# The front of the first feed-forward in smaller pieces, with its third batch mixed in the attention's tail

## What is computed

```python
x = x + _L0_attn_ref(_layernorm(x, axis=-1), ...)   # 16 heads of 8, rotary, masked by pages of 32 tokens, then @ wo
x = x + _L0_ffn_ref(_layernorm(x, axis=-1), ...)

def _L0_ffn_ref(x, gate_w, w1, b1, w2, b2, w3, b3, sw1, sw2, sw3):
    logits = xt @ gate_w.T
    scores = jax.nn.softmax(logits.astype(jnp.float32), axis=-1)
    top_vals, idx = jax.lax.top_k(scores, K)                  # K = 2 of E = 8 experts
    xs = xt[:, None, :] * weights[:, :, None]
    for e in range(E):
        mask = (idx == e).astype(x.dtype)
        h = jax.nn.silu(jnp.einsum('tkd,hd->tkh', xs, w1[e]) + b1[e])
        x2 = jnp.einsum('tkh,dh->tkd', h, w2[e]) + b2[e]
        x3 = jnp.einsum('tkd,hd->tkh', xs, w3[e]) + b3[e]
        y = y + jnp.sum(x2 * x3 * mask[:, :, None], axis=1)
    z = jax.nn.silu(xt @ sw1.T) * (xt @ sw2.T) @ sw3.T
    return (y + z).reshape(B, S, D)
```

## Time and profile before

| | |
|---|---|
| median of 3 runs | 1481.11 us (1480.87 to 1486.27) |
| the profiled execution | 1482.99 us, of which the span 1481.1 us |
| TensorE busy | 1214.6 us, 82% of the span |
| VectorE busy | 1153.7 us, 78% |
| ScalarE busy | 672.6 us, 45% |
| POOL busy | 653.5 us, 44% |
| mean granted TensorE clock | 0.907 of full speed |
| DMA | 120.37 MB, mean 81 GB/s |

### The profile page before, as it was taken

How to read it: one execution, slowest core, us unless ns; L and a number is a source line. 1 busy time by engine, 2 the same in 40 slices (tenths; PEclk the granted TensorE clock), 3 DMA queues, 4 the chain that set the end, 5 groups by cost and what they waited for, 6 DMA issues and landing times. The chain is left out here.

```text
span 1481.1 us, 21354 instructions
## 1 busy us (share of the span) xinstructions
PE 1214.6 (82%) x7478; PEld 548.8 (37%) x7478; DVE 1153.7 (78%) x1366; ACT 672.6 (45%) x1057; POOL 653.5 (44%) x468
## 2 busy tenths in 40 slices
PE   4937999998999789879978767877877867766998
PEld 2412334333344344444444212322322322355565
DVE  5868999998996256747556889999999999964554
ACT  2515999997897413212215783333333323302221
POOL 2320000101002166636743068989989989921000
PEclk9956999999999889989997868999999999995999
DMA  4321111312101443313520013343333333400331
GB/s 105 121 94 44 57 50 51 115 48 77 50 25 46 103 112 112 110 57 105 120 50 18 6 51 128 128 128 104 117 119 128 128 100 115 126 9 24 68 57 43
DMA packets 75346, 120.37 MB, mean 81 GB/s; under 512 B 13246, under 2 KB 42758, under 8 KB 75254
## 3 DMA queue, kind: packets, MB, share of 16 engines
q1 hardware_dynamic: 75254, 119.16, 27.2%
HBM read 105.09 MB, written 13.63 MB: 80 GB/s over the span
## 5 line engine op out<-in xcount | busy, mean ns | idle before, releaser
L635 DVE TENSOR_REDUCE att_found<-PS 128x2 f32<-128x1024 f32 (+2 forms) x288 | 333.2, 1219 | 17.9 <-PE PS L738 16.1
L705 ACT ACTIVATE att_prob<-PS 128x512 f32<-128x512 f32 x576 | 313.6, 596 | 42.5 <-PE PS L760 30.5
L1694 PE MATMUL PS<-ms_ch,ident_sb 128*128 128x512 f32 x512 | 269.0, 651 | 72.6 <-POOL ms_ch L1801 72.6
L1801 POOL TENSOR_TENSOR ms_ch<-xnT,ms_c_rows 128x1024 f32<-128x1024 f32 x128 | 304.8, 2392 | 41.3 <-DVE xnT L1759 21.3
L1759 DVE TENSOR_TENSOR_SCAN xnT<-ms_decay,PS 128x1024 f32<-128x1024 f32 x96 | 216.1, 2276 | 4.2
L779 PE MATMUL PS<-att_prob,att_v 128*32 128x256 f32 (+1 forms) x2560 | 183.9, 374 | 2.8 <-ACT att_out L694 2.6
L1694 PEld LDWEIGHTS PS<-ms_ch,ident_sb 128*128 128x128 f32 x512 | 98.6, 204 | 194.8 <-POOL ms_ch L1801 107.5
L1732 ACT ACTIVATE PS<-m_dt,m_a 128x1024 f32<-128x1024 f32 x32 | 35.8, 1118 | 260.5 <-DVE xnT L1759 260.5
L738 PE MATMUL PS<-kr,qr 55*128 55x128 bf16 (+4 forms) x1152 | 121.4, 292 | 30.8 <-PEq L260 15.6
L760 PE MATMUL PS<-qr,kr 55*128 55x128 bf16 (+4 forms) x1152 | 115.3, 278 | 15.5 <-ACT att_prob L705 9.1
L1746 DVE TENSOR_TENSOR PS<-ms_dtu,PS 128x1024 f32<-128x1024 f32 x96 | 114.7, 1213 | 6.8 <-PE PS L1685 6.7
(11 more groups left out here) (222 smaller groups left out, 1632.5 us busy)
## 6 DMA issues: line engine op xcount, KB each, us to landing
ms_c_rows<-bc_rows_dram SPq DMA_DIRECT2D x64, 512.0 KB, 5.9
f_gate_row<-gate_rows_dram SPq DMA_DIRECT2D x64, 256.0 KB, 3.4
ms_b_row<-bc_rows_dram SPq DMA_DIRECT2D x32, 512.0 KB, 3.6
f_mask_row<-mask_rows_dram SPq DMA_DIRECT2D x64, 128.0 KB, 3.0
qk_parts_dram<-qkv_parts SPq DMA_DIRECT2D x48, 128.0 KB, 1.9
heads_dram<-att_out SPq DMA_DIRECT2D x16, 256.0 KB, 2.7
f_mask_row<-mask_rows_dram SPq DMA_DIRECT2D x64, 64.0 KB, 3.3
...
```

The costliest lines, as they stand in the source:

```text
L635: dve.tensor_reduce(found[:, :, pair, first:first + (n - 1) * step + 1:step], PS[:, bank:bank + 2, :].rearrange("p r (w n) -> p r w n", w= ...
L705: act.activation(prob[:, step % PROB_RING * GH + h, :], PS[:, SCORE_BANK + unit % SCORE_RING, :], ACT.Exp, scale=float(D) ** -0.5).then_in ...
L1694: last = pe.matmul(PS[:, Y_BANK + 2 * half + q, :], g.ident[:, :], ch[:, half, q * CH:(q + 1) * CH], start=j == 0 and not odd, stop=j == J ...
L1801: pool.tensor_tensor(ch[:, half, :], h[:, odd, half, :], c_rows[:, s % C_RING, :], ALU.mult).then_inc(ch_ready, 1)
```

## The change

The front's operations are the same; their places, queues and PSUM banks change.

- **Heads of batch 2**: loaded by SyncE and divided by POOL in the attention's tail, mixed there in TensorE's last group (steps 4 and 6), added by VectorE there. Its moments, root and normalization come at the head of chunk 0, its turns at (0, 1) and (0, 2), its logits at (0, 4) and (0, 5).
- **Heads of batch 3**: sums loaded by ScalarE as the feed-forward begins, inverses stored at (0, 2), heads loaded at (0, 5), all by ScalarE's queue; divided at (1, 0) and (1, 1), mixed at (1, 3) and (1, 6), normalized at (2, 5) and (2, 6), turned at (2, 6) and (2, 7).
- **The search for the two best experts** is cut from two pieces of 5 and 7 operations into five of two or three (the last with the row tables); `add` and its statistics (`stat`) are apart, `moments` of batch 3 in two pieces, the logits in two halves.
- **Row tables** of batches 1 to 3 are written by ScalarE, not SyncE.
- Mixes of batch 2 use bank 0, of batch 3 bank 1, with waits for the bank's earlier reader; `out_sb` lives in the front.

```diff
@@ attend, SyncE
             f.store_inverses(sp, 2)
+            f.load_heads(sp, 2)
             f.store_row_tables(sp, 0)
             store(NG - 1)
-            f.store_row_tables(sp, 1)
@@ attend, POOL
-            for b in range(EARLY):
-                f.root(pool, b)
+            f.root(pool, 0)
+            for k in range(CPB):
+                f.divide(pool, 2, k)
+            f.root(pool, 1)
@@ attend, VectorE
             f.route_rows(dve, 0)
+            f.add(dve, 2, 0)
             f.route_scores(dve, 1)
+            f.stat(dve, 2, 0)
             f.route_weights(dve, 1)
...
             f.route_rows(dve, 1)
+            f.add(dve, 2, 1)
+            f.stat(dve, 2, 1)
@@ attend, TensorE
+                    if i == NG - 1 and k == 4:
+                        f.mix(pe, 2, 0)
                     if i == NG - 1 and k == 6:
                         f.turn_rows(pe, 0)
+                        f.mix(pe, 2, 1)
@@ Front
+    def mix_bank(self, b, k):
+        return (k, 2 + k, 0, 1)[b]
...
+        if b == 2 and k == 0:
+            pe.wait_ge(self.route_steps, self.SCORES)
+        if b >= 2 and k == 1:
+            pe.wait_ge(self.added, c)
@@ first_ffn, SyncE
-                    if (c, e) == (3, 7):
-                        f.store_row_tables(sp, 2)
-                    if (c, e) == (6, 0):
-                        f.store_row_tables(sp, 3)
...
-                    if (c, e) == (0, 3):
-                        f.load_heads(sp, 2)
-                        f.load_sums(sp, 3)
-                    if (c, e) == (1, 1):
-                        f.store_inverses(sp, 3)
-                    if (c, e) == (1, 4):
-                        f.load_heads(sp, 3)
@@ first_ffn, ScalarE
             act.preload_act_table(ACT.Silu)
+            f.store_row_tables(act, 1)
+            f.load_sums(act, 3)
             act.wait_ge(loaded, loads)
...
+                    if (c, e) == (0, 2):
+                        f.store_inverses(act, 3)
+                    if (c, e) == (0, 5):
+                        f.load_heads(act, 3)
@@ first_ffn, VectorE
+                for b, at in ((2, (1, 1)), (3, (4, 0))):
+                    if (c, e) == at:
+                        f.first_found(dve, b)
+                for b, at in ((2, (1, 2)), (3, (4, 1))):
+                    if (c, e) == at:
+                        f.first_marked(dve, b)
+                for b, at in ((2, (1, 5)), (3, (4, 2))):
+                    if (c, e) == at:
+                        f.second_found(dve, b)
...
+                for at, part in (((2, 5), 0), ((2, 6), 1)):
+                    if (c, e) == at:
+                        f.normalize(dve, 3, part)
...
+                if c == 0:
+                    f.moments(dve, 2)
                 shared(0)
+                if c == 0:
+                    f.normalize(dve, 2, 0)
                 third(0)
+                if c == 0:
+                    f.normalize(dve, 2, 1)
```

More of the change, by code:

```diff
@@ L659, in _ @@
                 f.add(dve, 0, k)
+                f.stat(dve, 0, k)
             f.moments(dve, 0)
@@ L809, in _ @@
                     if i == NG - 1 and k in (1, 5):
-                        f.logits(pe, k // 4)
+                        for part in range(CPB):
+                            f.logits(pe, k // 4, part)
+                    if i == NG - 1 and k == 4:
+                        f.mix(pe, 2, 0)
                     if i == NG - 1 and k == 6:
                         f.turn_rows(pe, 0)
+                        f.mix(pe, 2, 1)
             for v in range(NV):
@@ L853, with second_of_two @@
+def second_of_two(eng, steps, s, rank, tmp, w1, mask):
+    second_found(eng, steps, s, tmp, w1, mask)
+    second_ranked(eng, steps, rank, tmp, w1)
+    second_marked(eng, steps, rank, tmp, w1, mask)
 class Front:
@@ L880, with turn_bank, logits_bank, rows_bank @@
     BY_ROW = P // 2
[L882 to L884 removed]
+    def mix_bank(self, b, k):
+        return (k, 2 + k, 0, 1)[b]
+    def turn_bank(self, b, k):
+        return (k, 2 + k, k, 1 - k)[b]
+    def logits_bank(self, b):
+        return (0, 2, 0, 1)[b]
+    def rows_bank(self, b):
+        return (1, 1, 0, 1)[b]
     def tiles(self, b):
         return slice(TB * b, TB * (b + 1))
[L889 removed]
+    def load_sums(self, queue, b):
         for k in range(2):
[L892 to L893 removed]
@@ L895, in store_inverses @@
-    def store_inverses(self, sp, b):
-        sp.wait_ge(self.inverted, b + 1)
-        sp.dma_start(self.g.inverses[H * b:H * (b + 1), :, :].rearrange("h a (k t) -> (h a k) t", t=P), self.sums[:, b, :]).then_inc(self.inverse_out, 16)
-    def load_heads(self, sp, b):
-        sp.wait_ge(self.inverse_out, 16 * (b + 1))
+            queue.wait_ge(self.out_written[k], 16 * H // GH // 2 * (b + 1))
+        queue.dma_start(self.sums[:, b, :], self.g.heads[H * b:H * (b + 1), :, D, :].rearrange("h k (a t) -> h k a t", t=P)).then_inc(self.sums_in, 16)
@@ L901, in load_heads, with store_inverses @@
+    def store_inverses(self, queue, b):
+        queue.wait_ge(self.inverted, b + 1)
+        queue.dma_start(self.g.inverses[H * b:H * (b + 1), :, :].rearrange("h a (k t) -> (h a k) t", t=P), self.sums[:, b, :]).then_inc(self.inverse_out, 16)
+    def load_heads(self, queue, b):
+        queue.wait_ge(self.inverse_out, 16 * (b + 1))
         if b > 0:
-            sp.wait_ge(self.divided, CPB * b)
+            queue.wait_ge(self.divided, CPB * b)
         for k in range(CPB):
             heads, tokens = slice(H * b, H * (b + 1)), slice(k * CH, (k + 1) * CH)
-            sp.dma_start(self.num[:, k, :], self.g.heads[heads, k, 0:D, :]).then_inc(self.heads_in[k], 16)
@@ L906, in load_heads, with store_row_tables @@
-            sp.dma_start(self.inv[:, k, :], self.g.inverses[heads, :, tokens].to_broadcast([H, D, CH])).then_inc(self.heads_in[k], 16)
-    def store_row_tables(self, sp, b):
-        sp.wait_ge(self.rows_stored, 2 * (b + 1))
+            queue.dma_start(self.num[:, k, :], self.g.heads[heads, k, 0:D, :]).then_inc(self.heads_in[k], 16)
+            queue.dma_start(self.inv[:, k, :], self.g.inverses[heads, :, tokens].to_broadcast([H, D, CH])).then_inc(self.heads_in[k], 16)
+    def store_row_tables(self, queue, b):
+        queue.wait_ge(self.rows_stored, 2 * (b + 1))
@@ L1010, in turn_x, with logits @@
         pe.wait_ge(self.normed, CPB * b + k + 1)
+        if (b, k) == (2, 1):
+            pe.wait_ge(self.rows_stored, 4)
+        if (b, k) == (3, 1):
+            pe.wait_ge(self.rows_stored, 6)
         for j in range(TPC):
-            last = pe.transpose(self.g.PS[:, self.bank(b, k), j * P:(j + 1) * P], self.xn[:, k, j, :], self.g.ident[:, :])
+            last = pe.transpose(self.g.PS[:, self.turn_bank(b, k), j * P:(j + 1) * P], self.xn[:, k, j, :], self.g.ident[:, :])
         last.then_inc(self.transposed, 1)
-    def logits(self, pe, b):
-        if b == 0:
+    def logits(self, pe, b, k):
+        if b == 0 and k == 0:
             pe.wait_ge(self.e.route.loaded, self.e.route.all)
         pe.wait_ge(self.x_stored, CPB * (b + 1))
-        for n in range(TB):
+        for n in range(TPC * k, TPC * (k + 1)):
             at = T * b + P * n
-            last = pe.matmul(self.g.PS[:, self.bank(b, 0), n * NE:(n + 1) * NE], self.g.xnT[:, at:at + P], self.e.route.gate_w[:, :], start=True, stop=True)
+            last = pe.matmul(self.g.PS[:, self.logits_bank(b), n * NE:(n + 1) * NE], self.g.xnT[:, at:at + P], self.e.route.gate_w[:, :], start=True, stop=True)
         last.then_inc(self.logits_done, 1)
```

168 lines of the change are left out of this document (97 added, 71 removed).

## The result

| | before | changed |
|---|---|---|
| median of 4 runs each, side by side | 1482.72 us (1480.87 to 1486.27) | 1463.32 us (1458.86 to 1463.91) |
| profiled span | 1481.1 us | 1461.3 us |
| mean granted TensorE clock | 0.907 | 0.914 |

The ratio is 0.986, 95% interval 0.983 to 0.989: 19.4 us less between the medians, 19.8 between the spans. The forecast was 19.2 less and a time of 1462 us; 1463.32 was measured. The sum was right; its terms were less so.

The account below looks back on a forecast made before the run. TensorE was taken to bound undisturbed feed-forward chunks, with starved gate rows, batch 3's turns and VectorE lateness lengthening chunks 0 to 4. Terms 11.0 - 12.0 + 0.8 - 0.2 - 15.8 - 3.0 = -19.2 gave 1462 us, range 1450 to 1475.

Parts of the forecast that it names:

- signs named for a right forecast: Tail wait about 8 us; feed-forward 11 us later; chunk 0 near 33, chunk 3 near 29; batch 3's turns wait at most 3.
- The tail of the attention: longer, +11.0: Attention's tail: late normalization +8.1 us, two mixes +2.1, row tables leaving SyncE -1.2, slow clock +2.0.
- +2.0: Attention's tail: after 8.1 us of idleness TensorE runs at 1.2 GHz instead of 2.4, costing 2.0 us (ends 0 and 4).
- Chunk 0: -12.0: 44.8 us becomes 32.8: starved fifth row -10.2, moments' wait -2.6, slow clock -1.5, turns and logits +2.3.
- The pieces, chunk 1: 31.7: Chunk 1, +0.8 us: 27.2, mixes 2.1, and 2.4 for three VectorE pieces exceeding the 1.9 us free after a product.
- Chunk 2: 31.3: Chunk 2, -0.2 us: batch 3's turn waits 2.1 (half of 4.2), turns 1.0, moments 0.5, clock 0.5; ends -3 and +2.
- Chunk 3, -15.8: Chunk 3 keeps only the logits, 29.2 us; its 9.4 us wait, moments' stall, one mix and slow clock go.
- Chunk 4, -3.0: Chunk 4 has the second search in three pieces, 1.2 us over, and takes 28.4 us.
- Rival 1: Chunks 0 and 1: ScalarE's megabyte delays gate rows as SyncE's did, 3.7 us and little more: 1466 us; chance 0.12.
- Rival 2: Chunks 1, 2 and 4: split pieces each meet POOL afresh, normalizations cost their full 4.2 us, +9: 1471 us; chance 0.17.
- Rival 3: Attention's tail: heads land while TensorE still has work, so only mixes and barrier count, 0.9 us: 1452 us; chance 0.11.
- Rival 4: Attention's tail and chunk 0: clock stays at 1.2 GHz after the 8 us wait, +29 us: 1491 us; chance 0.05.

Follow-up runs that it names:

- run 5: Kernel before the change, with only the load of batch 2's heads moved to the attention's tail: 1478.83 us, ratio 0.9968.
- run 11: Kernel before the change, with batch 2's heads loaded in the attention's tail and also divided there, behind both roots: 1477.51 us, ratio 0.9958.
- run 1: Changed kernel with POOL's root of batch 1 put ahead of the two divisions of batch 2: 1456.24 us, ratio 0.9815.
- run 2: Changed kernel with batch 2's inverses stored and heads loaded one head group earlier, POOL's order kept: 1454.47 us, ratio 0.9802.
- run 6: Changed kernel with batch 3's sums, inverses and heads issued by SyncE instead of ScalarE, at nearly the same places: 1462.98 us, ratio 0.9871.
- run 7: Changed kernel with the search for the two best experts put back into two pieces, at the new places: 1464.92 us, ratio 0.987.
- run 9: Changed kernel with batch 2's inverses and heads issued one group earlier and both roots ahead of the divisions: 1459.88 us, ratio 0.9836.
- run 12: Run 9 plus one wait, so GpSimd divides batch 2 only after VectorE has normalized batch 1: 1453.94 us, ratio 0.9808.
- run 10: Changed kernel with GpSimd's sums of the products left out in chunk 2, so that chunk's output is wrong: 1466.26 us (one run).
- run 3: Changed kernel with the turns of batch 3 one step later, at (2, 7) and (3, 0): 1461.85 us, ratio 0.9851.
- run 8: Changed kernel with the turns of batch 3 at (2, 5) and (2, 6), in their normalization's step: 1474.35 us, ratio 0.9935.

## Why the prediction was right, and where its terms were not

- **What bounds the chunks** held. TensorE bounds chunks 1 and 3, gate rows the first half of chunk 0, VectorE's lateness chunk 2. Of the signs named for a right forecast one failed: the wait at the turns of batch 3 was 3.3 us, above the 3 allowed.
- **"The tail of the attention: longer, +11.0"**: 8.3. The 8.1 us of late normalization were 7.4: the inverses were there 1.85 us after their issue (474.14 to 475.99) instead of 2.4, and from there to the second division it was 6.8, as taken. The mixes cost 2.2 where 2.1 was priced, the shorter barrier gave 1.5 instead of 1.2. The term that failed is the clock, "+2.0". Low it was: the turns and the two units behind the wait are together 2.1 us longer than at full clock. But the last turn of the row tables (506.84, against 494.42 before, 2.5 taken off) came 9.9 us later, which is 7.4, 2.2 and only 0.3. That stretch of TensorE holds waits for ScalarE's exponentials in both kernels, and there I take the rest to have gone, which no run isolates.
- **"Chunk 0: -12.0"**: -11.2. Size right, attribution half right: I gave 10.2 of it to the starved row with its wait, clock and mixes as one block. Runs 5 and 11 split it, and the megabyte alone is 4.6.
- **"The pieces, chunk 1: 31.7"**: 28.9. The step that failed is the 2.4 for three pieces that pass the free 1.9 us by some 0.8 each. It priced a small operation at 1.33 us; most take 0.22, and only one that meets a running GpSimd operation takes more. Only the last piece passed 1.9, at 2.9 us, where no product was due, and TensorE waited 0.2 us for a product in the whole chunk.
- **"Chunk 2: 31.3"**: 35.9, the largest miss. Runs 1, 2, 6, 7, 9 and 12 leave this chunk's code alone and took 34.4 to 34.7, and run 7 tells the terms apart. Its granted clock was 1.00 behind the first wait, and it took 34.4 all the same. The two waits at the turns are 4.3 us together, the full 4.2 of which I took half on the idea that GpSimd might be at its idlest. It was not: the normalizations took 3.97 and 3.04 us, and the first began 0.9 late behind root 3. The wait for a product behind the moments was 1.6 where I had 0.5. These two terms are 3.3 of the 4.6. The low clock, for which I had 0.5, was 2.6 us in the changed kernel's profile, 1.0 to 1.4 in five of the other runs and none in run 7. The first microsecond of it costs nothing, since the second turn has to wait for VectorE anyway; only what is above it lengthened the chunk, by 1.5 us in the changed kernel. Run 10 shows most of the cause, run 3 that more distance does not help.
- **"Chunk 3, -15.8" and "Chunk 4, -3.0"**: -16.1 and, with chunk 5, -3.6. Run 8 confirms the core of it: with the turn in the same step as the normalization, TensorE waits 5.8 and 3.9 us again and 7.5 us come back, in chunk 2, where the turns now stand.
- **The rivals.** Rival 1, starvation by ScalarE's megabyte, did not come; the longest wait of GpSimd for a row, 3.4 us, lies ahead of that load. It is the fifth row again, 4.6 us after the fourth, 3.6 in run 6, which loads the sums elsewhere, and 5.9 in run 9 with the same code there; what delays it is open. Rival 2, dearer pieces, was right for the normalizations, which cost their full 4.2 as it says, and wrong for the search. Its rule, that an operation with two SBUF inputs or one like the normalization waits out GpSimd, is in the Trainium skill, SBUF — State Buffer, "Who interferes with whom", and by it runs 9, 10 and 12 agree: 3.98 against 2.14 for the same eight operations with and without a division beside them. Rival 3 is the kernel of run 2: one group earlier, the heads would have been hidden. The forecast for it was 1452, the measurement 1454.5. Rival 4: the clock was 1.00 from 492.1 us to the end of the attention and 0.95 in chunk 0, not 0.5.

So the total of -19.2 met -19.8 with help from misses that cancel: -2.7 in the tail and -2.8 in chunk 1 against +4.6 in chunk 2. That they cancel is luck; the mechanisms, a starved row, a late root in the tail and a turn too close to its normalization, are not.
